# Residual with tokens on partitions in the layer loop, embedding and first norm in one stage, new order of the lists

## The chip, the cores and the metric

The kernel runs on one core of a Trainium2 chip. The metric is device time of one execution in microseconds (us); the kernel before took 13516.87 us (median of 3 runs, 13515.38 to 13521.53). Five engines work side by side, each through its own list of instructions in order, and meet at semaphores: PE (TensorE, matmuls), DVE (VectorE), ACT (ScalarE), POOL (GpSimd) and SP (SyncE, which here only issues transfers). Transfers run on 16 DMA engines.

## The reference

16 images are cut into 196 patches each, embedded to 192 numbers, and joined with 128 text tokens: 16 sequences of 324 tokens. Then come a layernorm, 16 Mamba layers with a residual, a final rmsnorm added to the embedding, and a mixture of experts. Cut to what matters:

```python
h = concat([tok(x) @ W + b, txt], axis=1)             # 16 x 324 x 192
def mamba_layer(x, p):                                # 16 of them, one after the other
    u, z = split(rmsnorm(x, nw) @ in_w.T, 2)          # 384 channels each
    u = silu(causal_conv(u, cw, cb))
    dt_r, Bm, Cm = split(u @ xp_w.T, [48, 16, 16])
    dt = softplus(dt_r @ dtw.T + dtb)
    for t in tokens:                                  # 16 states per channel
        state = exp(dt[t] * A) * state + (dt[t] * u[t]) * Bm[t]
        y[t] = state @ Cm[t]
    return x + ((y + u * D) * silu(z)) @ ow.T
h = h + rmsnorm(layers(layernorm(h)), final_w)
h = h + experts(layernorm(h))                         # 16 experts, top 1080 tokens each
```

## The kernel before

**Stages.** `embed` (L86) multiplies the patches on PE, 8 chunks of inner patches first and 8 chunks of edges and corners after them, and leaves the sequences in `x_T`, with channels on partitions (2 x 96) and tokens along the row. `first_norm` (L221) is a block of its own: it stores `x_T` to DRAM and then computes the layernorm, with sums over channels made by matmuls with ones. `run_layers` (L375) is the long loop. Then come `scores_and_norm` (L1307; final norm, residual, second layernorm, gate), `shared_and_choice`, `place_tokens` and `experts`.

**The layer loop.** A unit is one sequence in one layer: 16 x 16 = 256 units. Each engine has a list for one step `u` (`tensor_step`, `scalar_step`, `vector_step`, `gpsimd_step`, `sync_step`), written out by hand. A step holds work of five units at once: `v[0]` is unit `u`, `v[1]` is `u + 1`, up to `v[4]`. Four early steps fill the pipeline. The lists are not cut off at the end, so the last step still works on units that do not exist.

**What a unit is.** The 16 states `s` are 16 scans on DVE (L924) of 128 x 972 elements. A scan needs its decay, `exp(dt * A)`, which ACT writes in three pieces into one of two PSUM halves (L709; `se_decay` waits until the scan before last has left its half), and its input, which POOL makes for two states at once (`ge_dbu`, L1000) into a ring `dbu` of `DRING` = 4 states. The scanned states are multiplied with C (`ve_product`, L932, on DVE; `ge_product`, L1009, on POOL for states 3 and 7, and for the first `SHARED[12]` = 4 of 6 slices of states 12 and 13), and PE adds them up (`te_sum`, L530). `ve_gate` (L941) multiplies by silu(z).

**The road of dt.** PE and ACT compute dt of a coming unit; POOL adds two corrections by accumulating transfers (`ge_add_terms`, L1019, then `ge_add_halves`, L1025), then multiplies dt by u (`ge_dtu`, L1031). SP stores dt and dt*u to DRAM (`sp_store_dt`, `sp_store_dtu`, L1094 and L1102) and reads them back, each row to four partitions: four loads `dt_rep` (L1108) and four loads `dtu_rep` (L1115) of 486 KB each, with small loads of B (`b_rep`, L1075) and C (`c_rep`, L1085) between them. `ge_dbu` for states 0 and 1 waits for `dtu_rep` 0 and 1, that for states 2 and 3 for `dtu_rep` 2 and 3. All of SP's transfers go through one queue in the order of its list.

**Order on POOL before** (a step): add_halves, dbu 10, dtu, dbu 12, product 7, dbu 14, `x_norm` (L949), dbu 0, product 12, dbu 2, dbu 4, product 3, add_terms, dbu 6, dbu 8. From the end of dtu to the start of dbu 2 it has six other instructions.

**The residual.** `te_out` (L567) adds the residual to the layer's output on PE, ACT copies it back to `x_T` (`se_out`, L739); the next layer's rmsnorm squares it on ACT, sums over channels on PE (`te_ss`, L610), and multiplies by the root on POOL (L949).

Of the kernel before, what the change touches and what calls it, by code (L numbers as in the profile page):

```python
# [15 lines left out]
B = 16  # L16
# [6 lines left out]
T = B * L  # L23
# [9 lines left out]
YW = IT * L // 2  # L33
NR = 4
RING = 8
DRING = 4
# [43 lines left out]

def raise_counts(eng, *sems):
    for s in sems:
        eng.sem_inc(s, BIAS)

def embed(nc, cst, x_T, ins, raw_tables):  # L86
# [4 lines left out]
    n_in = (G - 2) ** 2  # L91
    chunks = []
    for i in range(0, B, 2):
        chunks.append(("mid", "mid", i * n_in, 2 * n_in, i))
# [7 lines left out]
    assert at == B * PATCHES  # L102
    NX = 2 * n_in
# [15 lines left out]
    with ExitStack() as ctx:  # L119
# [10 lines left out]
        acc = ctx.enter_context(nc.psum_tensor("tok_acc", [HC, 4, BANK], F32))  # L130

        s_w = sem("s_tokw")
# [7 lines left out]

        with nc.Block() as block:
            @block.sync
            def _(sp):
                sp.dma_start(w[:, :, :, :].rearrange("p k c d -> p (k c d)"), tok_w).then_inc(s_w, 16)
                sp.dma_start(bias[:, :], tok_b).then_inc(s_w, 16)
# [3 lines left out]
                for c in range(2):  # L149
                    sp.dma_start(x_T[:, c, :].rearrange("p (b t) -> p b t", b=B)[:, :, PATCHES:L],  # L150
                                 text[c]).then_inc(s_txt, 16)
                sp.wait_ge(s_txt, 32)

            @block.vector
            def _(dve):
# [4 lines left out]
                dve.wait_ge(s_w, 32)  # L160
                done = 0
                for q in range(4):
                    hy, hx = q // 2, q % 2
# [13 lines left out]

            @block.tensor
            def _(pe):
                pe.wait_ge(s_v, 20)  # L180
                for i, (r, c, at, n, image) in enumerate(chunks):
                    pe.wait_ge(s_x[i % 2], 16 * (i // 2 + 1))
                    for half in range(2):
                        wait(pe, s_ev, 2 * i + half - 3)
                        for kc in range(8):
                            hy, hx = kc // 4, kc // 2 % 2
# [5 lines left out]
                        mm.then_inc(s_mm, 1)  # L192

            @block.scalar
            def _(act):
# [9 lines left out]
                act.wait_ge(s_w, 32)  # L205
# [10 lines left out]

NG = 4

def first_norm(nc, cst, x_T, h_rows):  # L221

    with ExitStack() as ctx:
        def sem(name):
            return ctx.enter_context(nc.semaphore(name))

        sq = [ctx.enter_context(nc.sbuf_tensor(f"ln_sq{i}", [HC, 2, L], F32)) for i in range(2)]
        rs = [ctx.enter_context(nc.sbuf_tensor(f"ln_rs{i}", [HC, L], F32)) for i in range(NG)]
        ps = ctx.enter_context(nc.psum_tensor("ln_ps", [HC, 2 * NG, BANK], F32))
        s_st = [sem(f"s_ln_store{g}") for g in range(B // NG)]  # L230
        s_sum, s_cen, s_sq = sem("s_ln_sum"), sem("s_ln_centred"), sem("s_ln_squares")
        s_var, s_log, s_rs, s_out = sem("s_ln_var"), sem("s_ln_log"), sem("s_ln_rs"), sem("s_ln_out")
        ones96 = cst["ones96"]

        def tokens(b):
            return slice(b * L, b * L + L)

        def total(b):
            return ps[:, b % (2 * NG), 0:L]

        with nc.Block() as block:
            @block.sync
            def _(sp):
                kept = h_rows.rearrange("p (c t) -> p c t", c=2)
                for g in range(B // NG):
                    at = slice(g * NG * L, (g + 1) * NG * L)
                    sp.dma_start(kept[:, :, at], x_T[:, :, at]).then_inc(s_st[g], 16)
                for stored in s_st:
                    sp.wait_ge(stored, 16)

            @block.tensor
            def _(pe):
                def mean(b):
                    wait(pe, s_log, b - 2 * NG + 1)
                    for half in range(2):
                        mm = pe.matmul(total(b), ones96[:, :], x_T[:, half, tokens(b)], start=(half == 0), stop=(half == 1))
                    mm.then_inc(s_sum, 1)

                def variance(b):
                    pe.wait_ge(s_sq, b + 1)  # L260
                    for half in range(2):
                        mm = pe.matmul(total(b), ones96[:, :], sq[b % 2][:, half, :], start=(half == 0), stop=(half == 1))
                    mm.then_inc(s_var, 1)

                for b in range(NG):
                    mean(b)
                for g in range(B // NG):
                    for b in range(g * NG, (g + 1) * NG):
                        if g == 0:
                            mean(b + NG)  # L270
                        variance(b)
                    for b in range((g + 1) * NG, min(B, (g + 2) * NG)):
                        if g > 0:
                            mean(b)

            @block.vector
            def _(dve):
                def centre(b):
                    dve.wait_ge(s_st[b // NG], 16)
                    dve.wait_ge(s_sum, b + 1)  # L280
                    for half in range(2):
                        dve.scalar_tensor_tensor(out=x_T[:, half, tokens(b)], in0=total(b), scalar=-1.0 / H,
                                                 in1=x_T[:, half, tokens(b)], op0=ALU.mult, op1=ALU.add).then_inc(s_cen, 1)

                def scale(b):
                    dve.wait_ge(s_rs, b + 1)
                    dve.tensor_tensor(x_T[:, :, tokens(b)], x_T[:, :, tokens(b)],
                                      rs[b % NG][:, :].unsqueeze(1).broadcast_to([HC, 2, L]), ALU.mult).then_inc(s_out, 1)

                for g in range(B // NG + 1):  # L290
                    for i in range(NG):
                        if g < B // NG:
                            centre(g * NG + i)
                    for i in range(NG):
                        if g > 0:
                            scale((g - 1) * NG + i)

            @block.scalar
            def _(act):
                def square(b):  # L300
                    act.wait_ge(s_cen, 2 * b + 2)
                    wait(act, s_var, b - 1)
                    act.activation(sq[b % 2][:, :, :], x_T[:, :, tokens(b)], ACT.Square).then_inc(s_sq, 1)

                def log(b):
                    act.wait_ge(s_var, b + 1)
                    wait(act, s_out, b - NG + 1)
                    act.activation(rs[b % NG][:, :], total(b), ACT.Ln, bias=cst["eps"][0:HC, 0:1], scale=1.0 / H).then_inc(s_log, 1)

                def root(b):  # L310
                    act.wait_ge(s_log, b + 1)
                    act.activation(rs[b % NG][:, :], rs[b % NG][:, :], ACT.Exp, scale=-0.5).then_inc(s_rs, 1)

                for g in range(B // NG + 1):
                    if g < B // NG:
                        for i in range(NG):
                            square(g * NG + i)
                    if g > 0:
                        act.preload_act_table_set(LOG_SET)
                        for i in range(NG):  # L320
                            log((g - 1) * NG + i)
                        act.preload_act_table_set(MAIN_SET)
                        for i in range(NG):
                            root((g - 1) * NG + i)
# [10 lines left out]
EXPS = (1, 0, 3, 2, 5, 4, 7, 6, 9, 8, 11, 10, 13, 12, 15, 14)  # L335
SCANS = (1, 0, 3, 2, 5, 4, 7, 6, 9, 8, 11, 10, 13, 12, 15, 14)
# [3 lines left out]
SUMS = (0, 2, 4, 6, 8, 10, 12, 14)  # L340
# [4 lines left out]
SHARED = {12: 4}  # L345
# [29 lines left out]
def run_layers(nc, cst, x_T, params, weights, b_rows, dt_rows, dtu_rows):  # L375

    ident, ones96, sel_c, fold = cst["ident"], cst["ones96"], cst["sel_c"], cst["fold"]
    with ExitStack() as ctx:
# [21 lines left out]
        sq = sb("sq", [HC, 2, L])  # L400
        rstd = sb("rstd", [HC, L])
# [5 lines left out]
        xp_rows = sb("xp_rows", [XROWS, L])  # L407
        c_rows = [sb(f"c_rows{i}", [80, L]) for i in range(2)]
# [7 lines left out]
        y_gated = sb("y_gated", [128, IT, L])  # L416
# [26 lines left out]
        s_ss = sem("s_ss")  # L443
# [22 lines left out]
        s_cq = sem("s_cq")  # L466
# [17 lines left out]
        def cols(unit):  # L484

            if isinstance(unit, int):
                return slice(unit % B * L, unit % B * L + L)
            return bass.ds(unit % B * L, L)
# [67 lines left out]
        def te_z(pe, p, par, half, freed):  # L556
            te_free(pe, freed)
            if half == 0:
                wait(pe, s_wz, 16 * (layer(p) + 1))
# [7 lines left out]
        def te_out(pe, u, half, freed):  # L567

            te_free(pe, freed)
            if half == 0:  # L570
                reached(pe, s_gate, u + 1)
                wait(pe, s_wo, 16 * (layer(u) + 1))
# [1633 lines left out]
```

## Time and profile before

| | us |
|---|---|
| median of 3 runs | 13516.87 |
| profiled execution: time | 13511.78 |
| profiled execution: first to last instruction (span) | 13510.0 |
| DVE busy in the span | 12701.1 (94%) |
| POOL busy | 12316.5 (91%) |
| PE busy | 12167.1 (90%) |
| ACT busy | 11039.5 (82%) |
| layer loop: first scan to the first instruction of the next stage | 275.59 to 12486.68 |

The shares of the whole span mix the layer loop with the stages around it, in which DVE and POOL are mostly idle. So the loop is read from windows inside it, and the order of work from the timeline of one unit.

### The profile page before, as it was taken

Reading aid. Unit: us, or ns where it says so; the run is one execution under the profiler, and the core shown is the slowest. Engines: PE = TensorE matmul, PEld = TensorE weight load, DVE = VectorE, ACT = ScalarE, POOL = GpSimd, SP = SyncE. Lnnn points to the kernel's source line nnn. Section 1 sums busy time; section 2 is a strip of 40 time slices with the busy share of each in tenths; the row PEclk is TensorE's granted clock in tenths of the full one; section 3 lists DMA queues with packets and bytes.
Section 4 is the critical chain, followed back from the end, with each engine's and each line's share of the span. In section 5 each row is a group of like instructions: output and inputs, shape, how many; then the busy total and the mean of one; then the engine's idle time right before and its main releaser. Section 6 shows DMA issues by size and latency. Waiting matters only on the chain. (4 is left out here: it accounts for less than half of the span.)

```text
span 13510.0 us, 194416 instructions
## 1 busy us (share of the span) xinstructions
PE 12167.1 (90%) x51470; PEld 6299.2 (47%) x51470; DVE 12701.1 (94%) x7474; ACT 11039.5 (82%) x21539; POOL 12316.5 (91%) x4049
## 2 busy tenths in 40 slices
PE   7999999999999999999999999999999999998899
PEld 4444444444444444444444444444444444444676
DVE  2999999999999999999999999999999999999543
ACT  4888888888888888888888888888888888888311
POOL 2999999999999999999999999999999999999033
PEclk8999999999999999999999999999999999999889
DMA  4555555555555555555555555555555555555122
GB/s 108 162 165 163 162 167 164 170 162 166 159 166 161 161 168 161 170 163 171 159 164 162 161 167 161 168 162 171 163 166 160 159 169 159 167 162 167 49 59 71
DMA packets 790402, 2092.82 MB, mean 155 GB/s; under 512 B 97429, under 2 KB 379989, under 8 KB 788177
## 3 DMA queue, kind: packets, MB, share of 16 engines
q1 hardware_dynamic: 693936, 1687.84, 36.3%
q0 software_dynamic: 95664, 403.36, 15.1%
q8 instruction: 50, 0.82, 0.0%
q10 hardware_dynamic: 720, 0.55, 0.0%
q14 instruction: 32, 0.25, 0.0%
HBM read 1418.92 MB, written 287.73 MB: 126 GB/s over the span
## 5 line engine op out<-in xcount | busy, mean ns | idle before, releaser
L1000 POOL TENSOR_TENSOR dbu<-dtu_rep,b_rep 128x1944 f32<-128x1944 f32 x2053 | 8989.4, 4391 | 161.1 <-DVE h L924 152.3
L924 DVE TENSOR_TENSOR_SCAN h<-ps,dbu 128x972 f32<-128x972 f32 x4103 | 8780.6, 2216 | 76.2 <-ACT ps L709 75.8
L709 ACT ACTIVATE ps<-dt_rep,A_cur 128x323 f32<-128x323 f32 x12312 | 5868.2, 522 | 1071.2 <-DVE h L924 1018.9
L530 PE MATMUL ps<-h,fold 128*32 128x486 f32 x16392 | 3743.2, 576 | 298.5 <-DVE y_gated L941 298.5
L932 DVE TENSOR_TENSOR h<-h,ps 128x1944 f32<-128x1944 f32 (+2 forms) x2050 | 3627.8, 1787 | 2.8 <-PE ps L517 2.8
L1009 POOL TENSOR_TENSOR h<-h,c_rep 128x972 f32<-128x972 f32 (+1 forms) x769 | 1956.0, 2544 | 0.0
L530 PEld LDWEIGHTS ps<-h,fold 128*32 128x32 f32 x16392 | 798.5, 109 | 2269.1 <-issue 2040.9
L600 PE MATMUL ps<-u_raw,w_cv 128*128 128x162 f32 (+7 forms) x8256 | 1800.5, 371 | 2.6 <-ACT u_raw L745 1.3
L600 PEld LDWEIGHTS ps<-u_raw,w_cv 128*128 128x128 f32 x8256 | 1358.3, 190 | 547.3 <-issue 206.0
L562 PE MATMUL ps<-x_norm,w_z 96*128 96x324 f32 (+1 forms) x4128 | 990.8, 383 | 146.4 <-ACT rstd L777 124.8
L587 PE MATMUL ps<-x_norm,w_u 96*128 96x324 f32 (+1 forms) x4128 | 991.2, 384 | 49.3 <-issue 45.3
L562 PEld LDWEIGHTS ps<-x_norm,w_z 96*128 96x128 f32 x4128 | 664.4, 190 | 720.5 <-ACT rstd L777 347.1
L575 PE MATMUL ps<-y_gated,w_o 128*96 128x324 f32 x3072 | 921.8, 435 | 0.0
L587 PEld LDWEIGHTS ps<-x_norm,w_u 96*128 96x128 f32 x4128 | 665.4, 191 | 515.6 <-issue 283.8
L517 PE MATMUL ps<-c_rows,sel_c 16*128 16x324 f32 x2052 | 829.3, 483 | 2.6 <-DVE h L932 2.6
L619 PE MATMUL ps<-u_act,w_x 128*128 128x324 f32 x1548 | 489.5, 452 | 344.7 <-ACT u_act L760 340.3
L626 PE MATMUL ps<-xp_rows,w_dt 128*128 128x162 f32 (+1 forms) x2064 | 561.3, 395 | 128.8 <-ACT sums L807 127.6
L575 PEld LDWEIGHTS ps<-y_gated,w_o 128*96 128x96 f32 x3072 | 500.4, 163 | 337.4
L949 POOL TENSOR_TENSOR x_norm<-x_norm,rstd 96x648 f32<-96x648 f32 x259 | 429.4, 1658 | 211.2 <-ACT rstd L781 211.2
L1031 POOL TENSOR_TENSOR terms<-sums,u_act 128x972 f32<-128x972 f32 x257 | 607.2, 2363 | 3.6 <-DMA sums<-sums 3.6
L573 PE MATMUL ps<-x_T,ident 96*96 x1024 | 401.2, 473 | 206.8 <-ACT x_T L739 206.8
L619 PEld LDWEIGHTS ps<-u_act,w_x 128*128 128x128 f32 x1548 | 272.8, 189 | 650.9 <-issue 565.7
(186 smaller groups left out, 11574.4 us busy)
## 6 DMA issues: line engine op xcount, KB each, us to landing
dtu_rep<-dtu_rows SPq DMA_DIRECT2D x1028, 486.0 KB, 4.8
dt_rep<-dt_rows SPq DMA_DIRECT2D x1028, 486.0 KB, 5.9
sums<-terms POOLq DMA_DIRECT2D x258, 972.0 KB, 6.7
b_rep<-b_rows SPq DMA_DIRECT2D x1028, 162.0 KB, 4.1
sums<-sums POOLq DMA_DIRECT2D x257, 486.0 KB, 4.5
dt_rows<-sums SPq DMA_DIRECT2D x257, 486.0 KB, 2.8
dtu_rows<-terms SPq DMA_DIRECT2D x257, 486.0 KB, 3.1
c_rep<-b_rows SPq DMA_DIRECT2D x770, 162.0 KB, 5.0
```

Source lines behind the costliest of these rows:

```text
L517: pe.matmul(c_ps, sel_c[64:80, q, :], c_rows[par][64:80, :], start=True, stop=True).then_inc(s_cbc, 1)
L530: mm = pe.matmul(y_ps[32 * r:32 * r + 32, half, :], fold[:, :], flat(h, step)[:, half * YW:(half + 1) * YW], start=(s < NR), stop=(s == la ...
L562: mm = pe.matmul(pj[:, lo:hi], w_z[:, c, it * 128:it * 128 + 128], x_norm[par][:, c, t:t + hi - lo], start=(c == 0), stop=(c == 1))
L575: mm = pe.matmul(pj[0:HC, 0:L], w_o[:, it, half * HC:(half + 1) * HC], y_gated[:, it, :], start=False, stop=(it == IT - 1))
L587: mm = pe.matmul(pj[:, lo:hi], w_u[:, c, it * 128:it * 128 + 128], x_norm[par][:, c, t:t + hi - lo], start=(c == 0), stop=(c == 1))
L600: mm = pe.matmul(pj[:, lo + skip:hi], w_cv[:, it * KC + KC - 1 - back, :], u_raw[:, it * L + t + skip - back:it * L + t + hi - lo - back], ...
L619: mm = pe.matmul(pj[0:XROWS, 0:L], w_x[:, it, :], u_act[par][:, it, :], start=(it == 0), stop=(it == IT - 1))
L709: ins = act.activation(decay[s % 2][:, it * L + 1:(it + 1) * L], dt_rep[:, s % NR, it, 1:L], ACT.Exp, scale=A_cur[:, it * N + s:it * N + s ...
L924: dve.tensor_tensor_scan(flat(h, s), decay[s % 2], flat(dbu, s), 0.0, ALU.mult, ALU.add).then_inc(s_scan, 1)
L932: dve.tensor_tensor(steps(h, s, n)[:, mine, :], steps(h, s, n)[:, mine, :], each(c_ps, n)[:, mine, :], ALU.mult).then_inc(s_prod, 1)
L1000: pool.tensor_tensor(steps(dbu, s, 2), steps(dtu_rep, r, 2), each(b_rep[:, q, :], 2), ALU.mult).then_inc(s_dbu, 1)
L1009: pool.tensor_tensor(steps(h, s, n)[:, mine, :], steps(h, s, n)[:, mine, :], each(c_rep[:, at, :], n)[:, mine, :], ALU.mult).then_inc(s_pp ...
```

## The change

- **Residual.** `x_T` in the loop becomes `x_R`, with tokens on partitions (108 x 3 chunks x 192). The rmsnorm's sum over channels becomes a sum along the row: `se_sq` is three ACT squares with a running sum, `se_log_ss` and `se_rstd` work on 108 x 3 numbers, `se_scaled` is three ACT copies with a scale. `te_turn` (six PE transposes) turns the result back, and ACT evicts it with the norm's weight (`se_x_norm`). `te_ss` on PE and the multiplication on POOL (L949) are gone. `te_out` has the tokens as output rows (two parts, nine matmuls of 192 columns and two with the identity).
- **Buffers.** The gate is written in place into `z_act`, `xp_rows` is double, the copy of C rows on ACT is gone, `DRING` is 6.
- **`SHARED[12]`** is 5 in place of 4: one slice (324 elements) of product 12 moves from DVE to POOL.
- **Lists.** All five lists are in a new order. `v[1]` now does nearly all of its scans in one step; the transfers of dt and B for `v[2]` are issued in the step before the one that uses them.
- **Embedding and first norm** are one block, `embed_and_norm`: edges first, inner chunks after them; per sequence, PE transposes to PSUM, DVE takes mean and variance (`bn_stats`, `bn_aggr`), ACT the root, DVE normalises into `x_R`. The weights come in four quarters, the store to DRAM is per chunk.
- **`scores_and_norm`** takes the squares and the scaling on ACT with tokens on partitions, turns on PE, and does the weight and the residual in one DVE instruction per half. The experts' weights lie in the room of `x_R`.

The diff, cut:

```diff
-DRING = 4
+DRING = 6
-SHARED = {12: 4}
+SHARED = {12: 5}
+FORMER = {0: 12 - N, 2: 14 - N, 4: 10 - N}
-EXPS = (1, 0, 3, 2, 5, 4, 7, 6, 9, 8, 11, 10, 13, 12, 15, 14)
+EXPS = (0, 1, 2, 3, 4, 5, 6, 7, 8, 9, 11, 10, 13, 12, 15, 14)
-SUMS = (0, 2, 4, 6, 8, 10, 12, 14)
+SUMS = (0, 2, 4, 6, 8, 10, 14, 12)
...
         def gpsimd_step(pool, u, par):
             if on[1]:
+                ge_dbu(pool, v[1], 2)
+                ge_dbu(pool, v[1], 4)
+                ge_dbu(pool, v[1], 6)
+                ge_dbu(pool, v[1], 8)
+            if on[2]:
+                ge_add_terms(pool, v[2])
+            if on[1]:
+                ge_product(pool, v[1], 3)
+                ge_dbu(pool, v[1], 10)
+            if on[2]:
+                ge_add_halves(pool, v[2])
+            if on[1]:
+                ge_dbu(pool, v[1], 12)
+            if on[2]:
+                ge_dtu(pool, v[2], q[2])
+            if on[1]:
+                ge_product(pool, v[1], 7)
+                ge_dbu(pool, v[1], 14)
+                ge_product(pool, v[1], 12)
+            if on[2]:
+                ge_dbu(pool, v[2], 0)
...
         def sync_step(sp, u, par, due=()):
+            if on[1]:
+                sp_load_dt(sp, v[1], 3)
+                sp_load_dtu(sp, v[1], 2)
+                sp_load_c(sp, v[1], q[1], 0)
+                sp_load_dtu(sp, v[1], 3)
+            if "c" in due:
+                reload_c(sp, u + 2)
...
+                sp_load_c(sp, v[1], q[1], 2)
+                sp_load_dt(sp, v[1], 2)
+                sp_load_b(sp, v[1], q[1], 3)
+                sp_load_c(sp, v[1], q[1], 1)
...
+            if on[2]:
+                sp_load_b(sp, v[2], q[2], 2)
+                sp_load_b(sp, v[2], q[2], 0)
+                sp_store_dt(sp, v[2])
+            if "u" in due:
+                reload_u(sp, u + 3)
+            if on[2]:
+                sp_store_dtu(sp, v[2])
+                sp_load_dtu(sp, v[2], 1)
+                sp_load_dtu(sp, v[2], 0)
+                sp_load_dt(sp, v[2], 0)
+                sp_load_b(sp, v[2], q[2], 1)
+                sp_load_dt(sp, v[2], 1)
```

DVE's new list of a step, in words: scans 14 and 15 and products 12 and 14 of `v[0]`; scans 0, 1, 2, product 0, scan 3, product 2, scan 4 of `v[1]`; the gate of `v[0]`; scans 5, 6, 7, product 4, scans 9, 8, 11, product 6, scans 10, 13, 12, products 8 and 10 of `v[1]`. ACT's new list of a step: copy of A, silu(z) of `v[1]`, second half of the convolution and silu of `v[2]`, decay 0, `se_xp`, decay 1, first half of dt, decay 2, second half of dt, decay 3, `se_x_norm`, `se_exp_x`, decay 4, `se_log`, `se_one_plus`, `se_z`, `se_lost`, decay 5, `se_z`, decay 6, `se_less` (after which POOL may issue add_terms), then the other decays with the copies between them. PE's new list around it: the second half of `te_dt`, `te_turn`, `te_sum` 14, `te_z`, `te_sum` 12.

## Rows read from the trace of the kernel before

**Rows 1.** Windows: us, busy of PE, PEld, DVE, ACT, POOL, PEclk, DMA share, GB/s.

```profile
0.00:136.00 136.00, 103.00 (x512) 80.49 (x512) 11.34 (x24) 17.31 (x35) 0.20 (x4) 0.95 0.51 109
136.00:198.00 62.00, 42.44 (x128) 23.00 (x128) 25.32 (x48) 35.52 (x56) 0.00 (x0) 0.83 0.20 65
2000.00:6000.00 4000.00, 3616.64 (x14960) 1789.19 (x14960) 3999.53 (x2102) 3510.95 (x6809) 3950.60 (x1262) 1.00 0.54 164
```

**Rows 2.** Groups by line and form, 2000 to 12000 us: busy us, mean ns.

```profile
L924 DVE TENSOR_TENSOR_SCAN h<-ps,dbu 128x972 f32<-128x972 f32 x3363 | 7195.6, 2215 | 1.3 <-ACT ps L709 1.1
L932 DVE TENSOR_TENSOR h<-h,ps 128x972 f32<-128x972 f32 x420 | 501.1, 1193 | 0.0
L932 DVE TENSOR_TENSOR h<-h,ps 128x648 f32<-128x648 f32 x210 | 180.0, 857 | 0.0
```

**Rows 3.** Timeline of DVE and ACT at the loop's two ends: start us, us.

```profile
275.59 6.48 DVE L924 TENSOR_TENSOR_SCAN h<-ps,dbu 128x972 f32<-128x972 f32 x3 [74.72 <-ACT ps L709]
12478.19 2.25 DVE L924 TENSOR_TENSOR_SCAN h<-ps,dbu 128x972 f32<-128x972 f32 x1
12486.68 1.38 ACT L1425 ACTIVATE f_sqx<-x_T 96x648 f32<-96x648 f32 x2 [7.44 <-PEq L1224]
```

**Rows 4.** Timeline of POOL in one unit: start us, us, instruction.

```profile
5999.59 0.85 POOL L1019 DMA_DIRECT2D sums<-terms  x1
...
6008.92 0.94 POOL L1025 DMA_DIRECT2D sums<-sums  x1
...
6014.07 2.35 POOL L1031 TENSOR_TENSOR terms<-sums,u_act 128x972 f32<-128x972 f32 x1
6016.26 4.42 POOL L1000 TENSOR_TENSOR dbu<-dtu_rep,b_rep 128x1944 f32<-128x1944 f32 x1
6020.54 2.33 POOL L1009 TENSOR_TENSOR h<-h,c_rep 128x972 f32<-128x972 f32 x1
6022.74 4.40 POOL L1000 TENSOR_TENSOR dbu<-dtu_rep,b_rep 128x1944 f32<-128x1944 f32 x1
6027.02 1.64 POOL L949 TENSOR_TENSOR x_norm<-x_norm,rstd 96x648 f32<-96x648 f32 x1
6028.54 4.38 POOL L1000 TENSOR_TENSOR dbu<-dtu_rep,b_rep 128x1944 f32<-128x1944 f32 x1
6032.80 3.02 POOL L1009 TENSOR_TENSOR h<-h,c_rep 128x1296 f32<-128x1296 f32 x1
6035.70 4.39 POOL L1000 TENSOR_TENSOR dbu<-dtu_rep,b_rep 128x1944 f32<-128x1944 f32 x1
```

**Rows 5.** Timeline of SP's queue in the same unit: start us, us of issue.

```profile
6016.64 0.32 SPq L1102 DMA_DIRECT2D dtu_rows<-terms  x1
...
6020.78 0.51 SPq L1115 DMA_DIRECT2D dtu_rep<-dtu_rows  x1
...
6028.93 0.51 SPq L1108 DMA_DIRECT2D dt_rep<-dt_rows  x1
```

**Rows 6.** These three issues: KB, us to landing; the window 6027 to 6030.

```profile
dtu_rows<-terms SPq DMA_DIRECT2D x1, 486.0 KB, 3.2
dtu_rep<-dtu_rows SPq DMA_DIRECT2D x1, 486.0 KB, 4.1
dt_rep<-dt_rows SPq DMA_DIRECT2D x1, 486.0 KB, 6.1
6027.00:6030.00 3.00, 3.00 (x14) 1.01 (x13) 3.00 (x3) 2.99 (x7) 3.00 (x3) 1.00 1.02 399
```

**Rows 7.** ACT before a decay; transposes and the final norm after the loop.

```profile
6036.48 1.44 ACT L709 ACTIVATE ps<-dt_rep,A_cur 128x323 f32<-128x323 f32 x3 [0.80 <-DVE h L924]
...
L1972 PE MATMUL e_ps<-ident,e_rows 108*128 108x108 f32 x192 | 31.2, 287 | 19.5 <-DMA e_rows<-n_rows,index 12.2 <-ACT e_x L2017 7.2
L1492 DVE SCALAR_TENSOR_TENSOR x_T<-x_T,fw,f_rsx 96x324 f32<-96x324 f32 x32 | 15.9, 546 | 49.2 <-ACT f_rsx L1435 49.2
```

More of the change, by code:

```diff
@@ L148, in _ @@
                     sp.dma_start(x_in[i % 2][:, :, 0:n], patches[:, :, at:at + n]).then_inc(s_x[i % 2], 16)
[L149 to L152, printed above, removed]
+                    if i == 1:
+                        for h in range(2):
+                            sp.dma_start(x_T[:, h, :].rearrange("p (b t) -> p b t", b=B)[:, :, PATCHES:L],
+                                         text[h]).then_inc(s_txt, 16)
+                    if i == N_EDGE + 1:
+                        sp.wait_ge(s_txt, 32)
+                    if i >= N_EDGE + 2:
+                        store(i - 2)
+                store(N_EDGE + B // 2 - 2)
+                store(N_EDGE + B // 2 - 1)
+                sp.wait_ge(s_st, 16 * (B // 2))
             @block.vector
@@ L192, in _ @@
                         mm.then_inc(s_mm, 1)
+                        if i > N_EDGE:
+                            turn(2 * (i - N_EDGE - 1) + half)
+                turn(B - 2)
+                turn(B - 1)
             @block.scalar
@@ L215, in _ @@
                         act.activation(out, src, ACT.Identity, bias=bias[:, half:half + 1]).then_inc(s_ev, 1)
[L218 to L324, printed above, removed]
@@ L327 @@
+                        if i > N_EDGE:
+                            root(2 * (i - N_EDGE - 1) + half)
+                root(B - 2)
+                root(B - 1)
 MAIN_SET = "natural_log_exp_and_others"
@@ L482, in run_layers, with of_unit, chunk @@
                                               sem("s_wd"))
[L484 removed]
+        def of_unit(unit, first, n):
             if isinstance(unit, int):
[L487 to L488 removed]
+                return x_R[:, unit % B * ROW + first * H:unit % B * ROW + (first + n) * H]
+            return x_R[:, bass.ds(unit % B * ROW + first * H, n * H)]
+        def chunk(c):
+            return slice(c * TS, (c + 1) * TS)
         def layer(unit):
@@ L565, in te_z, with te_out, te_turn @@
             return s_zev, 2 * p + half + 1
-        def te_out(pe, u, half, freed):
+        def te_out(pe, u, par, part, freed):
+            te_free(pe, freed)
+            if part == 0:
+                reached(pe, s_gate, u + 1)
+                wait(pe, s_wo, 16 * (layer(u) + 1))
+            first, n = OUTS[part]
+            pe.matmul(pj[0:TS, 0:n * H], ident[0:TS, 0:TS], of_unit(u, first, n), start=True, stop=False)
+            for c in range(first, first + n):
+                at = (c - first) * H
+                for it in range(IT):
+                    mm = pe.matmul(pj[0:TS, at:at + H], z_act[par][:, it, chunk(c)], w_o[:, it, :],
+                                   start=False, stop=(c == first + n - 1 and it == IT - 1))
+            mm.then_inc(s_out, 1)
+            return s_oev, 2 * u + part + 1
+        def te_turn(pe, j, half, freed):
             te_free(pe, freed)
             if half == 0:
-                reached(pe, s_gate, u + 1)
-                wait(pe, s_wo, 16 * (layer(u) + 1))
-            pe.matmul(pj[0:HC, 0:L], ident[0:HC, 0:HC], x_T[:, half, cols(u)], start=True, stop=False)
-            for it in range(IT):
-                mm = pe.matmul(pj[0:HC, 0:L], w_o[:, it, half * HC:(half + 1) * HC], y_gated[:, it, :],
-                               start=False, stop=(it == IT - 1))
-            mm.then_inc(s_out, 1)
-            return s_oev, 2 * u + half + 1
+                reached(pe, s_xw, j + 1)
+            for c in range(TPL):
+                mm = pe.transpose(pj[0:HC, chunk(c)], scaled[:, c, half * HC:(half + 1) * HC], ident[0:TS, 0:TS])
+            mm.then_inc(s_xt, 1)
+            return s_xn, 2 * j + half + 1
         def te_u(pe, k, par, half, freed):
@@ L733, in se_z, with se_out @@
             act.copy(half_of(z_pre, half), pj).then_inc(s_zev, 1)
-        def se_out(act, u, half):
-            reached(act, s_out, 2 * u + half + 1)
+        def se_out(act, u, part):
+            reached(act, s_out, 2 * u + part + 1)
             act.sem_inc(s_held, 1)
-            act.copy(x_T[:, half, cols(u)], pj[0:HC, 0:L]).then_inc(s_oev, 1)
+            first, n = OUTS[part]
+            act.copy(of_unit(u, first, n), pj[0:TS, 0:n * H]).then_inc(s_oev, 1)
         def se_ur(act, k, half):
@@ L1111, in sp_load_dtu @@
         def sp_load_dtu(sp, v, r):
-            reached(sp, s_dbu, turn(INPUTS, v - 1, (12 + r) // 2 * 2))
+            reached(sp, s_dbu, turn(INPUTS, v - 1, last(INPUTS, range(r // 2 * 2, N, NR))))
             sp.sem_inc(s_go, 1)
-            wait(sp, s_dst[1], 16 * (v + 1))
+            landed(sp, s_dst[1], v + 1)
             sp.dma_start(dtu_rep[:, r, :, :].rearrange("p i t -> p (i t)"),
@@ L1454, in exp_gate @@
                     act.activation(score_tiles(b), logits(b), ACT.Exp, scale=-1.0).then_inc(s_ge, 1)
-                for b in range(GS):
-                    square_x(b)
                 for g in range(N_G + 1):
-                    now, last, more = g < N_G, g > 0, g + 1 < N_G
+                    now, last = g < N_G, g > 0
+                    if now:
+                        for i in range(GS):
+                            square_x(GS * g + i)
                     act.preload_act_table_set(LOG_SET)
@@ L1467, in _ @@
                     act.preload_act_table_set(MAIN_SET)
+                    if last:
+                        for i in range(GS):
+                            root_n(GS * (g - 1) + i)
                     if now:
@@ L1470, in _ @@
                             root_x(GS * g + i)
-                    if last:
                         for i in range(GS):
-                            root_n(GS * (g - 1) + i)
+                            scale_x(GS * g + i)
+                    for i in range(GS):
+                        if last:
+                            exp_gate(GS * (g - 1) + i)
                     for i in range(GS):
```

600 lines of the change are left out of this document (309 added, 291 removed).

## The prediction, as it was made

> **What bounds the kernel now.** I read the windows first, because the shares of the whole span mix the layer loop with other stages. In the window from 2000 to 6000 us DVE is busy 3999.53 of 4000 and POOL 3950.60; ACT has 489 us of idle time and PE 383, at a full clock [rows 1]. So in the loop DVE never waits, POOL waits about 1%, and the other two have room. Next the groups by line, for the length of a unit: 3363 scans in 10000 us are 210.2 units of 16 scans, or **47.58 us a unit**, and DVE's wait before them is 1.3 us in all [rows 2]. Then the two ends of the loop: first scan at 275.59, next stage at 12486.68 [rows 3], so 12211 us, which are 256 x 47.58 = 12180 and 31 for the ends. Last the timelines of POOL and of SP in one unit [rows 4 to 6], since a list of transfers that is moved shows only there.
>
> All of the time is DVE's own work, so an edit that takes work off ACT, PE or POOL gains nothing in the loop. DVE must lose work, and the new lists must not make it wait.
>
> **DVE's work.** The only edit that takes work off DVE is SHARED[12] from 4 to 5. Products of 972 and of 648 elements take 1193 and 857 ns [rows 2], so one slice of 324 is 0.336 us, and DVE's unit falls to **47.24**. Over 256 units that is -86 us. The gate in place costs the same as before.
>
> **POOL's work.** From start to start, dbu takes 4.28, a product of 972 elements 2.20, the old product 12 2.90, x_norm 1.52 and dtu 2.19 [rows 4]. A slice more is 2.90 - 2.20 = 0.70. x_norm goes and a slice comes, so POOL loses 0.8 us a unit of work and has about 1.1 us of slack against 47.24. By work alone it is no bound. Its order is another matter.
>
> **The new cycle through POOL, SP and DRAM.** This is where I expect the loss. Before, six instructions stood between the end of dtu and the start of dbu 2: 6035.70 - 6016.26 = 19.4 us [rows 4]. In the new list there are four: product 7, dbu 14, the longer product 12 and dbu 0, together 2.20 + 4.28 + 3.60 + 4.26 = 14.3 us. In that time dtu has to be stored, the store has to land, and `dtu_rep` 2 and 3 have to land, which stand behind other loads. SP's list from the store on: dtu 1, dtu 0, dt 0, b 1, dt 1, then of the next step dt 3, dtu 2, c 0, dtu 3. These are seven large loads and two small ones, in one queue. Their price:
> - From dtu's end to the issue of its store 6016.64 - 6016.26 = 0.38 us [rows 4, 5]; the store lands 3.2 later [rows 6]; SP's answer to that I estimate at 0.2, from the 0.38.
> - The nine loads. The first lands 4.1 after its issue [rows 6]. Back to back the queue moved 399 GB/s at a DMA share of 1.02 [rows 6], so the engines are full; 486 KB then take 1.25 us and 162 KB 0.42. Six more large and two small give 4.1 + 7.5 + 0.8 = 12.4 us. The other end is what the old queue took for the same set, seven large and two small from the first `dtu_rep` to the third `dt_rep`: 6028.93 + 6.1 - 6020.78 = 14.3 us [rows 5, 6]. The new list issues all nine without a gap, so it is nearer to the back-to-back row: I take **12.8**.
> - POOL's own part of the circle, from dbu 2 to the end of dtu: six dbu, product 3, two issues of transfers, dtu: 25.7 + 2.2 + 1.8 + 2.2 = 31.9 us [rows 4].
>
> The circle is 31.9 + 0.38 + 3.2 + 0.2 + 12.8 = **48.5 us**, over DVE's 47.24 and over the old 47.58. It can't be shortened by running ahead, since each turn begins with the dbu that waits for the last load. With 12.4 it is 48.1, with 14.3 50.0. DRING = 6 doesn't help, because here POOL waits for a transfer and not for a scan. DVE then waits before scan 2, some 1.2 us a unit. 256 x (48.5 - 47.58) = **+236 us**.
>
> The Trainium skill, page "DMA: Bandwidth & Descriptors", section "Specifications", puts the ceiling of the path into SBUF at 435 GB/s; the row here shows 399. By that figure the ninth load would land an estimated 11.7 us after the first one's issue, the circle would be 47.4, and the sum about 13430, between the first rival below and the draw.
>
> **Other terms in the loop.** `reload_u` puts 288 KB ahead of the store of dtu once a layer: 0.74 us at 399 GB/s, 16 times, +12. The other reloads stand behind dtu 3, where their cover is the time until decay 2; without it, about 2 us a layer for the largest. At the end, the last step works on a unit that does not exist: before it did 7 scans and 2 products of the next unit, now 14 scans and 6 products, some 22 us more of DVE; the fill I take as equal within 10. Together +20.
>
> **ACT and PE.** The squares and copies by tokens replace a square of 648 and two copies of 324. Three pieces of 323 take 1.44 us [rows 7], so three of 192 cost no more than that, twice; against that the short logarithm and root and the copy of C rows that goes. Between -0.5 and +3 us a unit (the read-out of the running sums has no row); ACT's idle time of 489 us in the 84.1 units of the 4000 us is 5.8 us a unit [rows 1] and hides it. On PE the six transposes take 6 x 31.2 / 192 = 1.0 us [rows 7] in place of the sums with ones, and `te_out` stays about as long; idle there 4.6 us a unit [rows 1]. Taken at nothing in sum; where they stand in the lists is the second rival.
>
> **Ahead of the loop.** The two blocks take 198 us [rows 1]. In the joint block the norm runs beside the embedding; PE gets 96 transposes on top of its 103.0 us, 96 x 0.163 = 16 us [rows 1, 7]. Without any gain from the quarters of the weights the block is 136 + 16 = 152 us, with all of a quarter-wise start some 15 less, and the tail of the last sequence adds a few. I take 150: **-48**, between -35 and -60. Should the text loads, which now stand ahead of the third chunk, hold the edges up, that is in the range.
>
> **After the loop.** DVE waits 49.2 us for the roots of the final norm and works 15.9 on the scaling [rows 7]. The scaling and part of the wait go, and ACT gets the scaling instead, on the same chain: **-12**, between 0 and -25.
>
> **Sum.** +236 + 12 + 20 - 48 - 12 = +208. The profiled execution took 13511.78, 1.8 over its span and 5 under the median of the runs, so **13720**.
>
> **Rivals.**
> 1. *The loads land in time and DVE stays the bound* (faster). The point that decides is the landing of dtu 3: at 11.6 us or less after the first issue the circle is under 47.24. For it: 399 GB/s is one window of 3 us [rows 6], with stores and POOL's transfers in it, and the miss is under 1 us. Against it: the row of the full queue gives 12.4 at best. Then -86 + 20 - 60 = -126: **13385**.
> 2. *ACT's list binds.* With two decay halves a decay starts 0.80 us after its predecessors have left off and takes 1.44 [rows 7], of the 2.08 that the scan between covers; the new list puts dt, exp, log and the turned x into the same stretch, and scan 4 needs sum 12, which stands behind the second half of dt, a turn, sum 14 and z. A delay of 0.3 us a unit, if the loads are in time, is +77: **13460**. Idle time of 5.8 and 4.6 us speaks against more.
> 3. *A draw.* Loads at their fastest, around 12.0 us: the circle at 47.7 gives back what head and tail gain: **13510**.
> 4. *The old landing holds* (14.3): the circle at 50.0 would give 14090; I hold 13900 (49.2) for the reach of the range.
>
> **How the numbers follow.** The circle at over 47.8 has 0.60, with 13720 as its middle. Rival 1 has 0.22, rival 2 0.07, the neighbourhood of the draw 0.11, which splits into 0.03 faster and 0.08 same. This gives faster 0.32, same 0.08 and slower 0.60; 0.2%, 27 us, is about what a measurement of this kernel can tell from no change. The range goes from rival 1 with the full gain ahead of the loop, 13370, to the circle at 49.2, 13900, since leaving the rivals out would leave more than 2 in 10 out. Alone, the likeliest case has 13560 to 13900.
>
> **What would show it.** In the window 2000 to 6000 DVE should be busy about 97.5% and wait before a scan for POOL's dbu, and POOL should wait for the DMA `dtu_rep` about 2 us a unit, before one dbu in eight. If instead DVE is still at 100%, rival 1 holds. If DVE waits for ACT's decay, it is rival 2. In the timeline of SP the ninth load should land 12.4 to 14.3 us after the first one's issue. The first scan should come at about 228 in place of 275.59. The prediction is wrong if the new queue lands faster than the old one, or if POOL's list is entered at another place than dbu 2.

## The result and the profile after

The kernel after took **14499.04 us** (median of 4 runs, 14472.08 to 14513.29) against 13516.12 for the kernel before on the same chips: 1.0723 times, 95% interval 1.0708 to 1.0737. The forecast was 13720 with 13900 as the upper end of the range; the sign was right and the size was not.

| us | before | after | difference | forecast |
|---|---|---|---|---|
| profiled span | 13510.0 | 14496.9 | +987 | +208 |
| ahead of the loop, to the first scan | 275.59 | 229.64 | -46 | -48 |
| a unit of the loop, between scans 256 and 3840 | 47.60 | 51.52 | +3.92 | +0.9 |
| the loop less 256 units | 27 | 49 | +22 | +20 |
| from the loop's end on | 1023 | 1029 | +6 | -12 |

The ends are right to 20 us. What is wrong is the unit: 256 x 3.92 = 1004 us, of which I had forecast 236, and 12 more for a reload. First the window that answers to the last line of [rows 1]:

```profile
2000.00:6000.00 4000.00, 3452.62 (x14430) 1771.50 (x14430) 3689.58 (x1940) 3262.89 (x6819) 3589.04 (x1087) 0.95 0.49 153
```

DVE is busy 92.2% where it was 99.99%. The two ends of the loop, as in [rows 3], from the timelines of DVE and of ACT:

```profile
229.64 4.25 DVE L929 TENSOR_TENSOR_SCAN h<-ps,dbu 128x972 f32<-128x972 f32 x2 [77.72 <-POOL dbu L992]
...
13467.84 0.36 ACT L1425 ACTIVATE f_scx<-x_R 108x192 f32<-108x192 f32 x1 [13.49 <-PEq L1213]
```

Who waited for whom, from 2000 to 12000 us (in total, times, longest), 194 units:

```profile
POOL dbu L992 <- DMA dtu_rep<-dtu_rows: 527.5, 191, 7.5
DVE h L929 <- ACT ps L701: 455.9, 294, 5.0
...
ACT A_cur L707 <- issue: 381.9, 97, 5.2
...
ACT u_act L753 <- issue: 143.8, 95, 2.8
...
DVE h L929 <- POOL dbu L992: 191.2, 104, 5.0
...
DVE h L929 <- PE ps L519: 126.7, 118, 2.3
```

POOL waits 2.7 us a unit for `dtu_rep`; that is the forecast circle. But DVE's longest line is ACT's decay, and one line has no partner in the kernel before: ahead of the copy of A, which is the first instruction of ACT's list, ACT is idle 97 times, once in **two** units, 3.9 us each, for nothing that the profile shows ("issue"). A little later in the list, ahead of the silu that writes `u_act`, it is idle in the same way 95 times, 1.5 us each. A turn of the loop is two units, so this is one wait in two pieces, together 5.4 us, in every turn. The loop's own control instructions tell more. Line 1205 is the loop; these are its records between 6000 and 6110 us (engine, operation, ns, start):

```profile
L1205 DVEq COMPARE_BRANCH  x1: 56/56/56, 6032.6 to 6032.6; - x1
L1205 DVEq FUSED_REGOPS  x1: 74/74/74, 6032.9 to 6032.9; - x1
...
L1205 ACTq COMPARE_BRANCH  x1: 45/45/45, 6034.9 to 6034.9; - x1
L1205 ACTq FUSED_REGOPS  x1: 68/68/68, 6039.4 to 6039.4; - x1
...
L1205 POOLq COMPARE_BRANCH  x1: 45/45/45, 6039.7 to 6039.7; - x1
L1205 POOLq FUSED_REGOPS  x1: 68/68/68, 6039.9 to 6039.9; - x1
```

DVE and POOL go on 0.2 to 0.3 us after their branch, ACT 4.5 us after. The same records of ACT in the kernel before, where the loop is line 1216:

```profile
L1216 ACTq COMPARE_BRANCH  x2: 45/45/45, 6006.1 to 6101.2; - x2
L1216 ACTq FUSED_REGOPS  x2: 50/50/50, 6006.3 to 6101.5; - x2
```

Over the 112 turns from 400 to 12000 us ACT's gap is 3.7 to 6.4 us, in the median 5.2; in the kernel before it was 0.22 in every one of 121 turns. What comes in that time is code. The queues of the transfers, 2000 to 12000 us (packets, MB, share):

```profile
q1 hardware_dynamic: 495552, 1226.15, 34.1%
q0 software_dynamic: 55872, 289.67, 15.2%
q14 instruction: 545, 4.46, 0.1%
```

545 packets of 8192 bytes are 5.6 a turn; the kernel before had none in this window. ACT's turn has 290 instructions in the trace where it had 268. Three of the five packets come behind the branch; two come when ACT is at its 145th and its 272nd instruction, 127 apart.

SP has the same, once in 16 units, at its outer loop (line 1225; first and last of 12 turns):

```profile
L1225 SPq COMPARE_BRANCH  x12: 50/50/50, 2735.2 to 11810.9; - x12
L1225 SPq MOVE  x12: 41/41/41, 2740.6 to 11817.0; - x12
```

That is 5.4 and 6.1 us, in a list that after the change has its loop's end in the middle of the nine loads.

### The profile page after: what moved, and what is told of

Its sections match the earlier page's. It is cut to its first block and busy times, and to the rows that moved or that the text cites. A ratio compares the mean times of both kernels' runs of the same rounds, so it can differ in the third digit from the quotient of the medians.

```text
span 14496.9 us, 201406 instructions
## 1 busy us (share of the span) xinstructions
PE 12523.4 (86%) x53578; PEld 6698.8 (46%) x53578; DVE 12715.4 (88%) x7565; ACT 11130.0 (77%) x23496; POOL 12156.2 (84%) x3798
## 5 line engine op out<-in xcount | busy, mean ns | idle before, releaser
L519 PE MATMUL ps<-h,fold 128*32 128x486 f32 x16408 | 3998.7, 610 | 228.0 <-POOL h L1001 140.6
L937 DVE TENSOR_TENSOR h<-h,ps 128x1944 f32<-128x1944 f32 (+2 forms) x2054 | 3439.3, 1695 | 0.0
L1001 POOL TENSOR_TENSOR h<-h,c_rep 128x972 f32<-128x972 f32 (+1 forms) x771 | 2164.9, 2808 | 0.0
L614 PE MATMUL ps<-u_act,w_x 128*128 128x324 f32 x1548 | 640.7, 563 | 535.2 <-ACT u_act L753 530.8
L506 PE MATMUL ps<-xp_rows,sel_c 16*128 16x324 f32 x2054 | 830.8, 484 | 109.2 <-DVE h L937 108.4
L568 PE MATMUL ps<-w_o,z_act 128*108 128x192 f32 x4608 | 834.3, 326 | 0.0
L568 PEld LDWEIGHTS ps<-w_o,z_act 128*108 128x108 f32 x4608 | 759.4, 173 | 78.4 <-issue 3.9
L1011 POOL DMA_DIRECT2D sums<-terms x258 | 224.8, 871 | 624.8 <-ACT sums L835 552.1
L621 PEld LDWEIGHTS ps<-xp_rows,w_dt 128*128 128x128 f32 x2064 | 353.9, 205 | 659.2 <-ACT xp_rows L798 376.6
L579 PE MATMUL ps<-ident,scaled 108*96 108x108 f32 x1554 | 265.2, 283 | 405.9 <-ACT sums L810 363.8
```

Of the source, the lines that this page charges most:

```text
L519: mm = pe.matmul(y_ps[32 * r:32 * r + 32, half, :], fold[:, :], flat(h, step)[:, half * YW:(half + 1) * YW], start=(s < NR), stop=(s == la ...
L568: mm = pe.matmul(pj[0:TS, at:at + H], z_act[par][:, it, chunk(c)], w_o[:, it, :], start=False, stop=(c == first + n - 1 and it == IT - 1))
L614: mm = pe.matmul(pj[0:XROWS, 0:L], w_x[:, it, :], u_act[par][:, it, :], start=(it == 0), stop=(it == IT - 1))
L621: mm = pe.matmul(pj[:, lo:hi], w_dt[:, it * 128:it * 128 + 128], xp_rows[par][:, t:t + hi - lo], start=True, stop=True)
L937: dve.tensor_tensor(steps(h, s, n)[:, mine, :], steps(h, s, n)[:, mine, :], each(c_ps, n)[:, mine, :], ALU.mult).then_inc(s_prod, 1)
L1001: pool.tensor_tensor(steps(h, s, n)[:, mine, :], steps(h, s, n)[:, mine, :], each(c_rep[:, at, :], n)[:, mine, :], ALU.mult).then_inc(s_pp ...
```

## The experiments

**Theory.** ACT's longer list, shifted by new code ahead of it, no longer lies in the engine's instruction memory as a whole, so each turn waits for code; the circle of the prediction is a second, smaller cost under it. **Rival:** the idle time at the branch is an effect of something else, or the circle alone is slower than I thought.

### The place of the code on ACT, and on SP

```diff
+                for _ in range(40):
+                    act.sem_inc(s_pad, 1)
                 act.wait_ge(s_free, FREED)
                 all_units(scalar_step, act)
```

> The kernel after, with 40 more semaphore increments in ACT's list ahead of the layer loop, which take about 2 us once and do nothing else. Loop-back theory: ACT's loop body of 290 instructions, once in two units, now lies so that the jump back has to fetch code (8192-byte packets of the instruction queue, some 5 in two units; 5.2 us between the branch and the next instruction). Shifted by 40 the body fits again: the gap falls from 5.2 to 0.2 us, the instruction queue is almost empty in the loop, and the unit falls from 51.56 us to that of the circle through POOL, SP and DRAM, 48.6 (31.9 + 0.3 + 2.8 + 13.4 + 0.2), so about 13750 us, 13690 to 13830. If the stall is all there is and no circle, DVE is the bound at 47.24: about 13390. If the stall is an effect of something else (ACT waiting for PE, say), nothing changes: 14500.

Measured: 13932.5, ratio 1.0301 (1.0284 to 1.0318), **567 us less than after, from 40 instructions that do nothing**. The unit is 49.28. The waits and the queue (2000 to 12000 us):

```profile
POOL dbu L993 <- DMA dtu_rep<-dtu_rows: 510.0, 211, 7.2
DVE h L930 <- POOL dbu L993: 296.1, 192, 7.2
DVE h L930 <- ACT ps L702: 49.1, 68, 3.5
ACT A_cur L708 <- ACT ps L702: 40.0, 203, 0.2
```

```profile
q14 instruction: 61, 0.50, 0.0%
```

ACT's idle time ahead of its first instruction is 0.2 us and is a wait for its own decay, and the one ahead of `u_act` for nothing that the profile shows is gone; DVE now waits for POOL's dbu, as forecast. The time is over the expected range, so something was left.

```diff
+                for _ in range(88):
+                    sp.sem_inc(s_pad_sp, 1)
                 load_wu(sp, 0)
```

> As act_pad, and 88 semaphore increments ahead of SP's loop, which puts its outer loop (378 instructions, one turn in 16 units) where it lay in the kernel before. Loop-back theory: the 5.4 to 6.5 us that the jump back of the outer loop took, between dt 1 and dt 3 in the middle of the nine loads, go; each delays the ninth load by about 3 us in one unit, so 40 to 60 us in all under act_pad, 13700. If that delay is made up elsewhere, within 15 us of act_pad.

Measured: 13847.49, 1.0238 (1.0221 to 1.0255), 85 less, where 40 to 60 were expected; SP's longest gap at a branch falls from 6.7 to 0.3 us. So each of the 16 turns of that loop had cost over 5 us, nearly all of the stall.

To see whether it is the place in blocks of 128 that counts, act_sp_pad with more increments on ACT:

```diff
-                for _ in range(40):
+                for _ in range(129):
                     act.sem_inc(s_pad, 1)
```

> act_sp_pad with 129 increments ahead of ACT's loop in place of 40, so that the loop lies one block of 128 instructions further than in the kernel after. Code fetched in blocks of 128 (8192 bytes), of which three hold the loop without a fetch: the place in the block is that of the kernel after, the gap of 5 us comes back in every turn, about 14400. Blocks of 256, of which two are held: the loop lies in two, no fetch, 13850 as act_sp_pad.

Measured: 14503.3, 1.0728 (1.0707 to 1.075), the time of after, with its rows:

```profile
DVE h L930 <- ACT ps L702: 464.3, 307, 5.1
ACT A_cur L708 <- issue: 388.1, 97, 5.3
```

40 increments take the stall away and 129, which move the loop by 128, bring it back. So the place counts and not the length alone, and two places 128 apart behave alike, as blocks of 128 would have it. The 88 increments on SP are in this run too, and SP's gap is gone, yet the time is that of after and not the 14400 that was expected: while ACT stalls, SP's stall costs nothing that can be seen.

The same in the kernel before:

```diff
+                for _ in range(38):
+                    act.sem_inc(s_pad, 1)
                 act.wait_ge(s_free, FREED)
                 all_units(scalar_step, act)
```

> The kernel before, with 38 semaphore increments ahead of ACT's loop, so that its 268 instructions reach over one more block of 128. Loop-back theory: ACT then fetches code in every turn, and 5 us of stall in two units appear where there was 0.21 us. ACT had 5.8 us idle a unit, 11.6 in two, so that part is absorbed: 13540 to 14000, and the gap behind the branch and the instruction queue's packets show it whatever the time is. If the position of the code is of no account: 13517 within 10, with a gap of 0.21 us.

Measured: 14003.39, **1.0355** (1.0338 to 1.0372), just over the expected range, although nothing that computes was changed. The instruction queue, and ACT's first instruction (there `c_rows`):

```profile
q14 instruction: 505, 4.14, 0.1%
```

```profile
ACT c_rows L838 <- issue: 444.2, 101, 5.2
DVE h L925 <- ACT ps L710: 363.7, 114, 4.4
```

Here 2.3 to 3.2 us pass right behind the branch and the rest ahead of `c_rows`, 4.4 us of idle time in all. ACT's idle time of 5.8 us a unit did not absorb it: the decays come late at one place, and DVE, which had waited 1.3 us in all [rows 2], now waits 363.7 us for them. The stall alone explains a loss of half the size of the whole change.

### The circle, and what stood behind it

act_sp_pad has no code stall left, so the circle can be read there. POOL's timeline around one turn of it, then SP's issues with KB and us to landing (store at 6038.96, first load at 6041.61, ninth at 6047.73):

```profile
6006.77 17.13 POOL L993 TENSOR_TENSOR dbu<-dtu_rep,b_rep 128x1944 f32<-128x1944 f32 x4 [2.04 <-DMA dtu_rep<-dtu_rows]
...
6036.50 2.24 POOL L1024 TENSOR_TENSOR terms<-sums,u_act 128x972 f32<-128x972 f32 x1
6038.70 2.25 POOL L1002 TENSOR_TENSOR h<-h,c_rep 128x972 f32<-128x972 f32 x1
...
6048.77 4.33 POOL L993 TENSOR_TENSOR dbu<-dtu_rep,b_rep 128x1944 f32<-128x1944 f32 x1
6055.21 17.13 POOL L993 TENSOR_TENSOR dbu<-dtu_rep,b_rep 128x1944 f32<-128x1944 f32 x4 [2.11 <-DMA dtu_rep<-dtu_rows]
```

```profile
dtu_rows<-terms SPq DMA_DIRECT2D x1, 486.0 KB, 2.6
...
dtu_rep<-dtu_rows SPq DMA_DIRECT2D x1, 486.0 KB, 3.5
...
dtu_rep<-dtu_rows SPq DMA_DIRECT2D x1, 486.0 KB, 7.3
```

From dbu 2 to the end of dtu it takes 31.9 us; to the store 0.26; landing 2.6; the next issue at once; first load to ninth landing 6047.73 + 7.3 - 6041.61 = 13.4; to dbu 2 0.2. The sum is 48.4, and 55.21 - 6.77 = 48.44 is what the timeline has. The forecast circle was 48.5, with 12.8 for the loads, 3.2 for the store.

The trace also has the landing of each load. The first comes 3.5 us after its issue, where 4.1 was forecast; the second 2.55 after the first and the third 1.56 after the second, where 1.25 each was forecast; from then on a large one takes 1.2 and a small one 0.43 to 0.44. So the back-to-back row held once the queue was full, and not ahead of that (windows; the last two numbers are DMA share and GB/s):

```profile
6046.00:6047.00 1.00, 1.00 (x5) 0.68 (x5) 1.00 (x1) 0.99 (x2) 1.00 (x1) 1.00 0.40 128
...
6050.00:6051.00 1.00, 1.00 (x7) 0.20 (x4) 1.00 (x1) 1.00 (x1) 1.00 (x1) 1.00 1.01 412
```

Why the second load comes late was not looked into.

The unit of act_sp_pad is 48.93 on the mean, since one unit in 16 takes 51.9. There ACT waits for dt ahead of decay 2 (timeline of ACT):

```profile
3270.56 1.44 ACT L702 ACTIVATE ps<-dt_rep,A_cur 128x323 f32<-128x323 f32 x3 [3.69 <-DMA dt_rep<-dt_rows]
```

In that unit SP's list has the layer's `w_cv` ahead of dt 2, and `w_u` ahead of the store.

If the circle is the bound, bringing dtu 2 and dtu 3 forward must shorten it:

```diff
-                sp_load_dt(sp, v[1], 3)
                 sp_load_dtu(sp, v[1], 2)
-                sp_load_c(sp, v[1], q[1], 0)
                 sp_load_dtu(sp, v[1], 3)
+                sp_load_dt(sp, v[1], 3)
+                sp_load_c(sp, v[1], q[1], 0)
```

> act_sp_pad with two loads moved: in SP's list dtu 2 and dtu 3 come ahead of dt 3 and c 0, so that dbu 2 waits for seven loads in place of nine. Circle theory: the last of them lands 1.6 us earlier, the circle is 47.0, and DVE's own 47.24 is the bound: 13380 to 13440. If the circle is not what bounds act_sp_pad (ACT's or PE's list instead), within 40 us of act_sp_pad.

Measured: 13736.44, 1.0156 (1.0139 to 1.0173): 111 less where 400 to 470 were expected. DVE's wait for dbu has gone (0.8 us in all), but others took its place:

```profile
ACT ps L702 <- DMA dt_rep<-dt_rows: 315.3, 190, 4.6
...
DVE h L930 <- ACT ps L702: 128.7, 164, 3.5
...
DVE h L930 <- PE ps L520: 107.5, 92, 2.4
```

The wait is again for a transfer: dt 2, which now stands behind dt 3, c 0 and c 2. The expectation below names product 12, for which the issue of c 2 waits. SP's own waits show that one as small, 0.5 us each:

```profile
SPq L1072 <- POOL h L1002: 85.1, 169, 0.8
```

The landings show no trace of it: dt 3, c 0, c 2 and dt 2 land 1.23, 0.43, 0.44 and 1.23 us one after the other, as a full queue has them, and dt 2 some 7.2 us after its issue. So it is the place in the queue that makes dt 2 late, 3.3 us behind dtu 3. It was moved as well:

```diff
+                sp_load_dt(sp, v[1], 2)
                 sp_load_dt(sp, v[1], 3)
                 sp_load_c(sp, v[1], q[1], 0)
...
                 sp_load_c(sp, v[1], q[1], 2)
-                sp_load_dt(sp, v[1], 2)
```

> pads_dtu_first with dt 2 moved as well: SP's list of a step begins dtu 2, dtu 3, dt 2, dt 3, c 0, and then c 2. In pads_dtu_first ACT waited 1.5 us a unit for a dt_rep ahead of decay 2 (315 us in 206 units), since dt 2 stood behind c 2, which waits for POOL's product 12. Theory that the landings bound the loop, now that of dt 2: the wait goes and the unit falls from 48.5 to 47.3 or 47.6, 13430 to 13510. Theory that ACT's or PE's list is next (decay 0.7 us late, sum 12 late): 48.0 to 48.5, 13600 to 13740.

Measured: **13450.37, 0.9951 (0.9934 to 0.9967): 0.5% faster than the kernel before.** The unit is 47.37. The window, and DVE's waits from 2000 to 12000 us:

```profile
2000.00:6000.00 4000.00, 3594.99 (x15714) 1879.16 (x15713) 3993.15 (x2112) 3552.97 (x7436) 3913.88 (x1184) 1.00 0.53 165
```

```profile
DVE h L930 <- POOL dbu L993: 15.3, 35, 1.1
...
DVE h L930 <- ACT ps L702: 3.7, 13, 0.4
```

DVE is busy 99.8% again. To see that its work is now the bound, the slice of product 12 went back to it:

```diff
-SHARED = {12: 5}
+SHARED = {12: 4}
```

> pads_dt2_too with the slice of product 12 back on DVE (SHARED[12] = 4). If DVE's work is the bound by then: 0.336 us a unit more, 86 us slower than pads_dt2_too. If POOL's circle still is: 0.70 us a unit less, up to 180 us faster. If the decays are: within 30.

Measured: 13550.02, 1.0023 (1.0013 to 1.0034), 100 more, and 47.78 a unit: 0.41 where the slice is worth 0.336; the median unit goes from 47.25 to 47.59, by 0.34. DVE's work is the bound.

### Do the two causes add up?

The kernel after with the new order of loads (both diffs above) and without any increments:

> The order of loads of pads_dt2_too in the kernel after, without any increments ahead of the loops, so that ACT's jump back fetches code again. If the two causes add up as they did in the padded runs (567 and 85 for the code, 397 for the order), 13450 + 650 = 14100. If the new order leaves slack that takes the stall in, as the kernel before had it: less, down to the 490 that the stall cost there, 13940. If the stall only hurt by way of the late loads: near 13500.

Measured: 14323.12, 1.06 (1.0582 to 1.0617). The order alone gives 176 of its 397, and the code costs 873 under it. The stall is not hidden by slack in the loads; each expectation was too low. DVE waits 437.3 us for decays in this run, nearly what it did in after. So the two causes overlap: with the loads late, taking the code stall away gives 652 us (567 and 85), and with the loads in time 873.

The same order with the 40 increments on ACT, but not the 88 on SP:

> pads_dt2_too without the 88 increments on SP: the outer loop's jump back stalls SP 5 to 6.5 us once in 16 units, between dt 1 and dtu 2. With no slack in the circle this costs 3 to 5 us each time, 45 to 80 us: 13500 to 13530. If the new order has slack there: within 20 of 13450.

Measured: 13515.78, 1.0 (0.999 to 1.0009), 65 over pads_dt2_too: 4 us for each of the 16 turns. The longest waits show it (the last number of each line; POOL's longest was 1.8 in pads_dt2_too):

```profile
POOL dbu L993 <- DMA dtu_rep<-dtu_rows: 169.9, 205, 7.1
...
DVE h L930 <- POOL dbu L993: 72.2, 44, 6.6
```

## Why the prediction was wrong, and where it was right

- **What bounds the kernel, DVE's work.** Right. With the stalls and the late loads gone, most units take 47.2 to 47.3, where 47.24 was worked out, and DVE is the bound.
- **The circle.** Right, in its place, and in its sum: 48.4 measured where nothing else disturbs it, 48.5 forecast. That the sum came out to a tenth is luck: two of its terms were off by 0.6 each and cancelled, the loads with 13.4 in place of 12.8, the store with 2.6 in place of 3.2. I had leaned on the one window of a full queue, which tells nothing of the time until the queue is full; the row of the old queue, 14.3, was as near. Rival 1 needed 11.6 and falls, as do rivals 3 and 4.
- **The step that failed: "Taken at nothing in sum".** For ACT I counted what its instructions take and found room for them, 5.8 us a unit. I did not count the instructions, nor ask where the loop lies. With 22 more in a turn and at a new place, the engine waits for code in every turn, 5.4 us in two pieces at the head of its list, ahead of the decays, where the idle time of the rest of the turn is of no use. By padding alone this is 567 us of the 779 that were missing, and 85 more are the same on SP, once ACT's are gone. Length alone does not bring the stall: 290 instructions run without it in act_pad, and 268 have it in before_act_pad. Whether the longer turn or the new place would have brought it here by itself was not tested.
- **"The other reloads stand behind dtu 3, where their cover is the time until decay 2."** Wrong: dt 2, for decay 2, stands behind them, and has no cover left. Of act_sp_pad's mean of 48.93 some 4 us a layer, 65 in all, are the units at a layer's end, and I had put 12 for `reload_u`. With dt 2 ahead of `w_cv` (pads_dt2_too) those units take at most 47.8 on the mean.
- **A wait that no rival named.** Once dbu 2 had its input in time, decay 2 was late, by a load that stands too far back in a full queue. It is neither a list of ACT that is too dense (rival 2) nor the circle. The list of transfers had a second place with the same fault.
- **Ahead of the loop.** Right: -46, forecast -48.
- **After the loop.** Wrong, by 18 us. ACT got the scaling, and squares with a running sum (groups by line from 13460 to 13630 us, then a wait of the same stretch):

```profile
L1440 ACT ACTIVATE f_scx<-x_R,f_rsx 108x192 f32<-108x192 f32 x48 | 17.0, 439 | 0.0
L1425 ACT ACTIVATE f_scx<-x_R 108x192 f32<-108x192 f32 x48 | 16.6, 346 | 13.5 <-PEq L1213 13.5
...
L1425 ACT ACTIVATION_READ_ACCUMULATOR f_scx<-x_R 108x1 f32 x48 | 8.9, 186 | 0.0
...
L1501 DVE SCALAR_TENSOR_TENSOR x_T<-f_ps,fw,f_res 96x324 f32<-96x324 f32 x32 | 16.3, 549 | 43.6 <-PE f_ps L1375 43.5
```

```profile
DVE nrm L1512 <- ACT f_rsn L1456: 39.5, 4, 11.9
```

  42.5 us of ACT stand here, where it had 11.6 for the squares; the roots of this norm fall from 13.3 to 5.3, and ACT's work in the whole stage rises from 64.0 to 79.9. DVE did not lose the 15.9 of [rows 7]: it still has 16.3 in an instruction per half, and what went is the addition of the residual, 12.9. It now waits 39.5 for ACT's roots of the second norm, where it waited 6.2. That ACT's work sets the stage's length is argued from these waits, not shown by a run.
- **The last step.** Right: +22, forecast +20.

In sum: 14499 less 13720 is 779. Code on ACT 567, on SP 85, reloads some 55, the stage after the loop 18; the rest, some 50, is a unit of 48.6 to 48.7 in place of 48.5 and the ends. Without the code stalls (act_sp_pad) the time is 13847, inside the range that was stated, so the sign was no luck. The parts of code and loads are not independent, as act_pad_128 and dt2_no_pads show, so this sum holds for the order in which the causes were taken away.

## What to carry to other kernels

A list that is issued from a loop has a length and a place as well as a duration: after a change that adds instructions, or that moves code ahead of the loop, look at the time between the loop's branch and the next instruction of each engine, and at the packets of the instruction queue, before any other line. A circle through a queue of transfers can be summed from the kernel's own trace to a tenth of a microsecond; from the trace of another kernel its terms were off by 0.6 each. Then do the same for every load behind it in the list. Idle time that an engine has over a turn says little on its own: here 5.8 us a unit did not cover one wait of some 5 us at a place on which another engine depends.

## What the hardware showed that was not expected

- **TensorE's clock fell behind the waits, those for code and those for loads.** In the kernel before it was granted in full from 2000 to 6000 us [rows 1]. In after, PE ran out of work for 3.2 us (from 6042.35 to 6045.56), waiting for the `u_act` that ACT's code stall had made late, and the granted clock then fell to half, 1.2 GHz (windows; PEclk is the third from the end):

```profile
6029.00:6034.00 5.00, 4.99 (x24) 3.02 (x24) 5.00 (x3) 4.20 (x11) 5.00 (x3) 1.00 0.50 199
...
6045.50:6048.70 3.20, 3.15 (x6) 1.85 (x6) 0.47 (x2) 2.62 (x4) 0.00 (x0) 0.50 0.95 286
```

  The mean granted clock from 2000 to 12000 us is 0.95 in after, 0.96 with the code stalls alone (dt2_no_pads), 0.98 with the late loads alone (act_sp_pad) and 1.00 with neither (pads_dt2_too). DVE's waits for PE's sums are 126.7 us in after and 24.2 in act_sp_pad; what part of them is the clock's was not separated.
- **A running sum on ACT costs an instruction of its own,** 186 to 188 ns each, three for a unit and 48 after the loop.
